# A four-layer graph GRU on one core: the first steps of each layer, the work ahead of the flag and the last statistics put in another order

## The chip, the cores and the metric

The kernel runs on one core of one Trainium2 chip. The metric is the time of one execution on the device in microseconds (us). The kernel before takes 2390.28 us, the median of three runs from 2387.75 to 2390.46.

The engines are named as in the profile: PE multiplies matrices, DVE, ACT and POOL work on tiles of up to 128 partitions, and SP only issues DMAs here. Each engine runs its own instructions in order and waits on semaphores that the others raise.

## The reference

```python
h = x                                              # 50000 nodes x 128
for l in range(4):
    m = h @ weight[l]
    agg = segment_sum(m[src], dst, 50000)          # 75000 edges, sorted by dst; every node has an edge to itself
    gi, gh = agg @ w_ih.T + b_ih, h @ w_hh.T + b_hh
    r = sigmoid(gi_r + gh_r); z = sigmoid(gi_z + gh_z)
    n = tanh(gi_n + r * gh_n)
    h = (1 - z) * n + z * h
y = x + (h + x)
out = (y - mean(y)) / sqrt(var(y) + 1e-5)          # over the 128 features
```

## The kernel before

**Tiling.** The 50000 nodes are cut into 100 blocks of 500. A block's state is kept transposed, 128 features on the partitions and 504 columns (four groups of 125 nodes and one unused column each). Every layer goes over the 100 blocks, one step for a block. Steps are written out for the first ten and the last ten blocks of a layer and looped ten at a time between them. Products are made in fp32r in three passes, so each operand is split into a high part (a rounded copy, made by ACT) and a low part (the difference, made by DVE, or by POOL for the first half of h).

**One block's path.** POOL gathers the rows of the neighbours with three indirect DMAs (`gather`, L555). ACT rounds them (`high_gathered`, L832), DVE makes the remainder (`low_gathered`, L1089), PE sums them over the edges with a 0/1 selection matrix (`sum_edges`, L686), which ACT has widened from bytes (`widen`, L839). DVE adds h (`aggregate`, L1110; the final layer does that on PE instead), ACT and DVE split the result (`high_part` L844, `low_part` L1101). PE makes the products for r, for h's and for the input's part of n, and for z (L698). ACT makes r (`r_gate` L851), DVE `r_times_hn` (L1116) and `n_argument` (L1123), ACT the tanh (`n_gate` L855) and z (`z_gate` L859), DVE `difference` (L1127), `product` (L1133) and `new_state` (L1142). PE turns the new state back to rows (L733), ACT copies it out of PSUM (`rows_out` L865), SP stores it.

**The order.** It is written out by hand, per engine, in a `step` that works on several blocks at once: in step b, DVE and ACT work on r, n and z of block b, but already on the edge sums of block b+2 and on the gathered rows and h of block b+3. The start of a layer (`if first:`) therefore does this work for blocks 0, 1 and 2 before step 0. Steps wait for nothing but their data; every engine's list is fixed.

**Between layers.** A layer's gathers may read any row of the state that the layer before stored, so POOL waits for all stores (`s_store`) before the first of 15 gathers (five blocks). The h columns of the next layer's first five blocks are loaded in the last five steps already.

**Before layer 0** there is a set-up: DVE sorts each block's edges into slots (up to L1064, after which `V_TABLES` is reached), then a check on the edge lists is added up on PE and copied to `flag_i` (L1079). Every engine reads this flag and branches to `fast_path()` or `general_path()`. The inputs take the fast path.

**The end.** In the final layer the sum with x is made two steps later (`ROWLAG`), its statistics in groups of five blocks (`moments`, `squared_difference`, `variance`, then POOL's power L539 and `shift` L1181), and rows are normalised nine blocks later (`OUTLAG`), the first half of a block's columns on ACT (L873), the second half in the last nine blocks on DVE (`last_rows`, L1262).

## Time and profile before

| | |
|---|---|
| median of 3 runs | 2390.28 us |
| lowest, highest | 2387.75, 2390.46 us |
| the profiled execution's own time | 2411.64 us |
| its span, first to last instruction | 2409.9 us |
| mean granted clock of PE | 0.968 |
| PE, DVE busy | 93%, 93% of the span |
| ACT, POOL busy | 78%, 73% |
| set-up (before the flag) | 65.9 us |
| `r_times_hn` of block 0 in layers 0 to 3, at | 87.46, 677.78, 1233.37, 1788.91 us |
| median step of layers 0 to 3 (L1116 to L1116) | 5.65, 5.30, 5.30, 5.78 us |
| last `new_state` of layers 0 to 2, at | 655.88, 1210.76, 1764.82 us |
| last `new_state` to the end of the span | 2390.18 to 2409.9 us |

The profiled execution took 21.4 us more than the median. DVE and PE are busy for 93% of the span; the page's 40 slices fall below 9 tenths of DVE in the first two, at the three changes of layer (slices 11, 20 and 30) and in the last. In the profile "L1116" stands for `r_times_hn`, the first DVE instruction of every step, so the time from one L1116 to the next is the length of a step.

### The profile page before, as it was taken

The page shows a single profiled execution, that of the slowest core. Times are in us where ns is not written, and L with a number is a line of the kernel's source. Part 1 is how long each engine was busy: PE and PEld are TensorE (multiplying, and loading weights), DVE is VectorE, ACT ScalarE, POOL GpSimd, SP SyncE. Part 2 cuts the span into 40 slices and gives each one's busy share as a digit, 9 for nine tenths or more (in the row PEclk, how much of TensorE's full clock was granted, in tenths as well). Part 3 has the DMA queues.
Part 4 walks back from the last instruction along what each step waited for, and adds up shares of the span by engine and source line. Part 5 has one row for each costly group of instructions (what it writes and reads, how often), then busy time and mean ns, then how long its engine had stood idle before and what let it go on. Part 6 is the DMA issues. An engine that isn't in the chain of part 4 may idle for free.

```text
span 2409.9 us, 49779 instructions
## 1 busy us (share of the span) xinstructions
PE 2241.2 (93%) x11832; PEld 1880.0 (78%) x11832; DVE 2250.7 (93%) x4540; ACT 1871.1 (78%) x3592; POOL 1749.2 (73%) x1644
## 2 busy tenths in 40 slices
PE   1799999999879999999969999999969999999996
PEld 0688888888768888888858888888858878778885
DVE  7799999999869999999969999999949999999998
ACT  0588888888758888888758878888847888888886
POOL 1788888778577777777567777777648888888883
PEclk7799999999989999999989999999979999999998
DMA  1355555555535565655535565555534555555553
GB/s 35 104 161 160 155 159 156 159 154 159 153 109 171 170 173 167 173 171 170 167 107 171 169 173 169 170 171 169 171 106 121 152 149 150 149 149 151 152 150 110
DMA packets 277064, 363.68 MB, mean 151 GB/s; under 512 B 107754, under 2 KB 186586, under 8 KB 276980
## 3 DMA queue, kind: packets, MB, share of 16 engines
q1 hardware_dynamic: 238196, 310.43, 43.4%
q0 software_dynamic: 38784, 52.30, 9.2%
q8 instruction: 32, 0.52, 0.1%
q14 instruction: 52, 0.43, 0.1%
HBM read 209.32 MB, written 179.81 MB: 161 GB/s over the span
## 4 chain that ended last, share of the span: by engine, by line
DVE 37%; issue 24%; PE 24%; ACT 10%; DVEq 1%; DMA 1%; POOL 1%; another core or an unknown queue 0%; ACTq 0%; SPq 0%; POOLq 0%
PE pR L698 6%; DVE narg L1123 6%; PE pZ L698 6%; DVE a_lo L1101 5%; DVE diff L1133 4%; DVE diff L1127 4%; DVE bn L1158 3%; PE pHN L698 3%; PE pA L686 3%; DVE y_rows L1151 3%; DVE h_lo L1094 2%; PE pO L733 2%; DVE aggT L1110 2%; DVE narg L1116 2%; DVE sel L1083 2%
## 5 line engine op out<-in xcount | busy, mean ns | idle before, releaser
L555 POOL DMA_INDIRECT gath<-state,idx x900 | 925.7, 1029 | 235.5 <-issue 220.0
L533 POOL TENSOR_TENSOR h_lo<-hT,h_hi 128x252 fp32r<-128x252 f32 (+1 forms) x400 | 351.4, 879 | 260.8 <-DVE diff L1133 124.3
L555 POOL DMA_INDIRECT gath<-in_x_dram,idx x300 | 389.4, 1298 | 124.2 <-issue 121.8
L1116 DVE SCALAR_TENSOR_TENSOR narg<-pHN,bhh,rg 128x504 f32<-128x504 f32 x400 | 293.8, 734 | 17.0 <-ACT rg L851 7.1
L686 PE MATMUL pA<-sel,g_hi 128*128 128x168 f32 x1200 | 280.1, 267 | 31.0 <-DVE g_lo L1089 27.8
L686 PE MATMUL pA<-sel,g_lo 128*128 128x168 f32 x1200 | 292.9, 277 | 0.0
L851 ACT ACTIVATE rg<-pR,bsum 128x504 f32<-128x504 f32 x400 | 274.2, 686 | 21.3 <-PE pR L698 17.7
L1089 DVE TENSOR_TENSOR g_lo<-gath,g_hi 128x384 fp32r<-128x384 f32 x400 | 240.9, 602 | 44.2 <-ACT g_hi L832 42.0
L855 ACT ACTIVATE pA<-narg,bih 128x504 f32<-128x504 f32 x200 | 137.2, 686 | 184.9 <-DVE narg L1123 125.5
L855 ACT ACTIVATE pIN<-narg,bih 128x504 f32<-128x504 f32 x200 | 137.2, 686 | 182.2 <-DVE narg L1123 117.4
L859 ACT ACTIVATE zg<-pZ,bsum 128x504 f32<-128x504 f32 x400 | 270.3, 676 | 5.4 <-remote 4.4
L1133 DVE TENSOR_TENSOR diff<-zg,diff 128x504 f32<-128x504 f32 x400 | 269.1, 673 | 4.4 <-ACT zg L859 3.6
L686 PEld LDWEIGHTS pA<-sel,g_hi 128*128 128x128 f32 x1200 | 231.9, 193 | 49.0 <-issue 32.4
L733 PEld LDWEIGHTS pO<-ident,newT 128*125 128x125 f32 x1400 | 191.2, 188 | 75.1 <-issue 32.0
L839 ACT CAST sel<-sel 128x504 fp32r (+1 forms) x400 | 249.5, 625 | 0.0
L686 PEld LDWEIGHTS pA<-sel,g_lo 128*128 128x128 f32 x1200 | 232.5, 194 | 16.7
L832 ACT CAST g_hi<-gath 128x384 fp32r<-128x384 f32 x400 | 211.0, 527 | 39.7 <-DMA gath<-state,idx 38.3
L733 PE MATMUL pO<-ident,newT 128*125 128x128 f32 x1400 | 222.3, 281 | 14.7 <-DVE newT L1142 13.9
L1110 DVE TENSOR_TENSOR aggT<-pA,hT 128x504 f32<-128x504 f32 x300 | 200.8, 669 | 6.0 <-remote 5.1
L1101 DVE TENSOR_TENSOR a_lo<-aggT,a_hi 128x504 fp32r<-128x504 f32 x300 | 202.3, 674 | 4.1 <-ACT a_hi L844 2.7
L698 PE MATMUL pR<-a_hi,wf_hi 128*128 128x504 f32 x400 | 190.8, 477 | 0.5 <-DVE a_lo L1101 0.4
L844 ACT CAST a_hi<-aggT 128x504 fp32r<-128x504 f32 x300 | 179.5, 598 | 13.4 <-DVE aggT L1110 9.7
(185 smaller groups left out, 6464.0 us busy)
## 6 DMA issues: line engine op xcount, KB each, us to landing
columns<-newT SPq DMA_DIRECT2D x300, 252.0 KB
hT<-columns SPq DMA_DIRECT2D x300, 252.0 KB
state<-o_rows SPq DMA_DIRECT2D x300, 224.0 KB
x_rows<-in_x_dram SPq DMA_DIRECT2D x200, 224.0 KB
out_dram<-o_rows SPq DMA_DIRECT2D x100, 224.0 KB
gath<-state,idx POOLq DMA_INDIRECT x900
state<-o_rows SPq DMA_DIRECT2D x300, 26.0 KB
idx<-edge_src SPq DMA_DIRECT2D x395, 1.5 KB
```

What stands on the lines that cost most here:

```text
L533: nc.gpsimd.tensor_tensor(h_lo[:, u % RING, cols], hT[:, u % RING, cols], h_hi[:, u % RING, cols].bitcast(F32), ALU.subtract).then_inc(s_h ...
L555: pool.indirect_dma_start(out=gath[:, u % RING, j, :], out_offset=None, in_=states[l], in_offset=bass.IndirectOffsetOnAxis(ap=idx[:, u % R ...
L686: last = nc.tensor.matmul(to, rows, cols, start=begins, stop=ends)
L698: last = nc.tensor.matmul(bank, w, xx[:, u % RING, :], start=k == 0, stop=k == len(passes) - 1)
L733: last = nc.tensor.transpose(bank[0:ROWS, k * D:(k + 1) * D], newT[:, u % RING, k * CP:k * CP + ROWS], ident[:, :])
L839: nc.scalar.copy(sel[:, u % 2, :], sel8[:, bass.ds(b, 1), :].rearrange("p o c -> p (o c)")).then_inc(s_sel, 1)
L851: nc.scalar.activation(rg[:, :], pR[:, 0:COLS], ACT.Sigmoid, bias=bsum[:, 0:1]).then_inc(s_r, 1)
L855: nc.scalar.activation(n_bank(u), narg[:, :], ACT.Tanh, bias=bih[:, 2:3]).then_inc(s_n, 1)
L859: nc.scalar.activation(zg[:, :], pZ[:, 0:COLS], ACT.Sigmoid, bias=bsum[:, 1:2]).then_inc(s_z, 1)
L1101: v.tensor_tensor(a_lo[:, u % RING, :], sums_of if summed else aggT[:, :], a_hi[:, u % RING, :].bitcast(F32), ALU.subtract).then_inc(s_alo, 1)
L1116: v.scalar_tensor_tensor(narg[:, :], pHN[:, 0:COLS], bhh[:, 2:3], rg[:, :], ALU.add, ALU.mult).then_inc(s_t1, 1)
L1133: v.tensor_tensor(diff[:, :], zg[:, :], diff[:, :], ALU.mult).then_inc(s_e, 1)
```

## The change

1. **The start of a layer.** Before step 0 only block 0's edge sums are made (gathered rows split, sums, `aggregate`, `high_part`, `low_part`), with block 1's gathered rows split. Block 1's sums stand in step 0 behind the products of r and n, block 2's behind the z product and behind `product` and `z_gate` of block 0, and with them the gathered rows of block 3.
2. **h of the next layer.** `high_h`, `low_h` and `split_h` of the next layer's blocks 0, 1, 2 move into the last three steps of a layer (`on_from`, `PRE = 3`).
3. **Ahead of the flag.** SP loads the first five blocks of x before it waits for the flag; PE turns blocks 0 to 2, ACT copies and rounds them, POOL makes their low parts whole; POOL issues the first 15 gathers when `V_TABLES` is reached; DVE makes block 0's selection bytes between the checks and the flag. Temporaries of the set-up that lay in `hT` move to `y_rows`.
4. **The last statistics.** Those of the last five blocks are made as three (before the sums of the last two blocks) and two (`LATE = 2`). POOL's power and `shift` are divided likewise.

```diff
+PRE = 3
+LATE = 2
...
             def fast_path():
-                for u in range(RING):
-                    load_x(u, u)
...
+            for c in range(PRE):
+                split_h(0, c, c, None, True)
+            for c in range(RING):
+                gather(0, c, c, 0, False)
...
                     def step(i, u, first, last):
                         b = UNROLL * i + u
-                        if first:
-                            if l == 0:
-                                for c in range(RING):
-                                    gather(c, c, 0, False)
-                                    if c < 3:
-                                        split_h(l, c, c)
-                            else:
-                                for c in range(3):
-                                    split_h(l, c, c)
-                                for v in range(RING):
-                                    pool.wait_ge(s_store[v], 32 * TURNS * l)
-                                for c in range(RING):
-                                    gather(c, c, 0, True)
-                        if exists(i, u, 3):
-                            nb, nu, _ = after(i, u, 3)
-                            split_h(l, nb, nu, l * NB + b if exists_before(i, u, 1) else None)
+                        if first and l:
+                            for v in range(RING):
+                                pool.wait_ge(s_store[v], 32 * TURNS * l)
+                            for c in range(RING):
+                                gather(l, c, c, 0, True)
+                        coming = on_from(l, i, u, PRE)
+                        if coming:
+                            split_h(*coming[:3], l * NB + b if exists_before(i, u, 1) else None)
...
+            pe.wait_ge(s_v, V_WEIGHTS)
+            for c in range(PRE):
+                turn_h(c, c, s_xld[c % RING], 2, c == 0)
...
                             sum_edges(l, 0, 0, start)
+                        r_and_n_products(l, b, u, start,
+                                         l * NB + b - 1 if l or exists_before(i, u, 2) else None,
+                                         l < L - 1 and (l > 0 or exists_before(i, u, PRE)))
+                        if first:
                             sum_edges(l, 1, 1, False)
-                        r_and_n_products(l, b, u, start,
-                                         l * NB + b - 1 if l or exists_before(i, u, 2) else None, l < L - 1)
-                        if exists(i, u, 2):
+                        elif exists(i, u, 2):
                             sum_edges(l, *after(i, u, 2)[:2], False)
                         z_product(l, b, u, start)
+                        if first:
+                            sum_edges(l, 2, 2, False)
...
                         normal(i, u, 0)
+                        if first:
+                            high_part(l, 1, 1, final)
                         n_gate(l, b, u)
...
                         normal(i, u, 1)
+                        if first:
+                            high_gathered(2, 2, TURNS * l + 1)
+                            widen(l, 2, 2)
+                            high_part(l, 2, 2, final)
+                            high_gathered(3, 3, TURNS * l + 1)
+                            widen(l, 3, 3)
...
+            for j in range(TILES):
+                select(0, 0, j)
             dve.wait_ge(s_flag, 1)
...
+                        summed = after(i, u, 1 if first else 2)[:2] if exists(i, u, 2) else None
+                        if not final and summed:
+                            aggregate(l, *summed)
...
-                        if exists(i, u, 3):
+                        if not first and exists(i, u, 3):
                             low_gathered(l, *after(i, u, 3)[:2])
-                            if not final:
-                                low_h(l, *after(i, u, 3)[:2])
-                        if exists(i, u, 2):
-                            low_part(l, *after(i, u, 2)[:2], final)
+                        coming = on_from(l, i, u, PRE)
+                        if coming and coming[0] < L - 1:
+                            low_h(*coming[:3])
+                        if summed:
+                            low_part(l, *summed, final)
                         product(l, b, u)
...
+                        if first:
+                            low_gathered(l, 2, 2)
+                            if not final:
+                                aggregate(l, 2, 2)
+                            low_part(l, 2, 2, final)
+                            low_gathered(l, 3, 3)
...
-                        for k in range(ROWLAG, 0, -1):
+                        ahead = slice(RING, UNROLL - LATE), TURNS - 1
+                        late = slice(UNROLL - LATE, UNROLL), TURNS
+                        moments(*ahead, NB - LATE)
+                        squared_difference(*ahead)
+                        variance(*ahead)
+                        for k in range(LATE, 0, -1):
                             remainder(NB - k, UNROLL - k, GROUPS - 1)
                             row_stats(NB - k, UNROLL - k)
-                        whole = slice(RING, UNROLL), TURNS - 1
-                        moments(*whole, NB)
+                        moments(*late, NB)
...
```

ACT at the start of layer 1 before: block 2's widened matrix (`sel`) and gathered rows, block 1's sums, r of block 0 (`rg`), and so on to r of block 1 in the last row.

```order
L839 CAST sel<-sel 128x504
L832 CAST g_hi<-gath 128x384
L844 CAST a_hi<-aggT 128x504
L851 ACTIVATE rg<-pR,bsum 128x504
L828 CAST h_hi<-hT 128x504
L832 CAST g_hi<-gath 128x384
L839 CAST sel<-sel 128x504
L855 ACTIVATE pIN<-narg,bih 128x504
L844 CAST a_hi<-aggT 128x504
L859 ACTIVATE zg<-pZ,bsum 128x504
L851 ACTIVATE rg<-pR,bsum 128x504
```

And now, from the gathered rows of block 1 to r of block 1:

```order
L857 CAST g_hi<-gath 128x384
L876 ACTIVATE rg<-pR,bsum 128x504
L853 CAST h_hi<-hT 128x504
L869 CAST a_hi<-aggT 128x504
L880 ACTIVATE pIN<-narg,bih 128x504
L884 ACTIVATE zg<-pZ,bsum 128x504
L857 CAST g_hi<-gath 128x384
L864 CAST sel<-sel 128x504
L869 CAST a_hi<-aggT 128x504
L857 CAST g_hi<-gath 128x384
L864 CAST sel<-sel 128x504
L876 ACTIVATE rg<-pR,bsum 128x504
```

Between r of block 0 and r of block 1 ACT had three rounded copies of h, g and the sums, one matrix to widen, tanh and z. It now has h of block 3, the sums of block 1 ahead of the tanh, and behind z the rows of blocks 2 and 3, their two matrices and the sums of block 2.

DVE there before, from block 1's `aggregate` on, with `r_times_hn` of blocks 0 and 1 as the rows `narg<-pHN`:

```order
L1110 TENSOR_TENSOR aggT<-pA,hT 128x504
L1101 TENSOR_TENSOR a_lo<-aggT,a_hi 128x504
L1116 SCALAR_TENSOR_TENSOR narg<-pHN,bhh,rg 128x504
L1123 TENSOR_TENSOR narg<-pIN,narg 128x504
L1110 TENSOR_TENSOR aggT<-pA,hT 128x504
L1127 TENSOR_TENSOR diff<-hT,pIN 128x504
L1089 TENSOR_TENSOR g_lo<-gath,g_hi 128x384
L1094 TENSOR_TENSOR h_lo<-hT,h_hi 128x252
L1101 TENSOR_TENSOR a_lo<-aggT,a_hi 128x504
L1133 TENSOR_TENSOR diff<-zg,diff 128x504
L1116 SCALAR_TENSOR_TENSOR narg<-pHN,bhh,rg 128x504
```

And now, from `r_times_hn` of block 0 to that of block 1:

```order
L1149 SCALAR_TENSOR_TENSOR narg<-pHN,bhh,rg 128x504
L1156 TENSOR_TENSOR narg<-pIN,narg 128x504
L1143 TENSOR_TENSOR aggT<-pA,hT 128x504
L1160 TENSOR_TENSOR diff<-hT,pIN 128x504
L1127 TENSOR_TENSOR h_lo<-hT,h_hi 128x252
L1134 TENSOR_TENSOR a_lo<-aggT,a_hi 128x504
L1166 TENSOR_TENSOR diff<-zg,diff 128x504
L1122 TENSOR_TENSOR g_lo<-gath,g_hi 128x384
L1143 TENSOR_TENSOR aggT<-pA,hT 128x504
L1134 TENSOR_TENSOR a_lo<-aggT,a_hi 128x504
L1122 TENSOR_TENSOR g_lo<-gath,g_hi 128x384
L1149 SCALAR_TENSOR_TENSOR narg<-pHN,bhh,rg 128x504
```

Block 1's `aggregate` and `a_lo` moved behind `r_times_hn` of block 0, and behind `product` (`diff<-zg,diff`) there are four more instructions ahead of block 1's `r_times_hn`.

DVE at the very end of the final layer, from the last new state on, before:

```order
L1142 TENSOR_TENSOR newT<-diff,pA 128x504
L1151 SCALAR_TENSOR_TENSOR y_rows<-x_rows,pO 125x512
L1158 BN_STATS bn<-y_rows 125x6 x4
L1151 SCALAR_TENSOR_TENSOR y_rows<-x_rows,pH 125x512
L1158 BN_STATS bn<-y_rows 125x6 x4
L1163 TENSOR_TENSOR mv<-bn 125x20
L1164 SCALAR_TENSOR_TENSOR mv<-bn 125x20
L1165 TENSOR_TENSOR mv<-bn 125x20
L1169 SCALAR_TENSOR_TENSOR mv<-mv 125x20
L1175 SCALAR_TENSOR_TENSOR veps<-mv 125x20
L1262 TENSOR_SCALAR o_rows<-y_rows,rstd,nmr 125x128 x8
```

And now:

```order
L1175 TENSOR_TENSOR newT<-diff,pA 128x504
L1196 TENSOR_TENSOR mv<-bn 125x12
L1197 SCALAR_TENSOR_TENSOR mv<-bn 125x12
L1198 TENSOR_TENSOR mv<-bn 125x12
L1202 SCALAR_TENSOR_TENSOR mv<-mv 125x12
L1208 SCALAR_TENSOR_TENSOR veps<-mv 125x12
L1184 SCALAR_TENSOR_TENSOR y_rows<-x_rows,pO 125x512
L1191 BN_STATS bn<-y_rows 125x6 x4
L1184 SCALAR_TENSOR_TENSOR y_rows<-x_rows,pH 125x512
L1191 BN_STATS bn<-y_rows 125x6 x4
L1196 TENSOR_TENSOR mv<-bn 125x8
```

Five small instructions on 12 columns now stand ahead of the sums with x (`y_rows`) of the last two blocks, and those on 20 columns have become ones on 8.

## Rows read from the trace of the kernel before

**Rows 1.** The page, its first line.

```profile
span 2409.9 us, 49779 instructions
```

**Rows 2.** Timeline of DVE at the start of layer 1: start us, duration us, instruction [idle before].

```profile
654.28 0.68 DVE L1127 TENSOR_TENSOR diff<-hT,pA 128x504 f32<-128x504 f32 x1 [0.75 <-ACT pA L855]
655.06 0.68 DVE L1133 TENSOR_TENSOR diff<-zg,diff 128x504 f32<-128x504 f32 x1
...
667.51 0.56 DVE L1089 TENSOR_TENSOR g_lo<-gath,g_hi 128x384 fp32r<-128x384 f32 x1 [6.38 <-ACT g_hi L832]
671.37 0.56 DVE L1089 TENSOR_TENSOR g_lo<-gath,g_hi 128x384 fp32r<-128x384 f32 x1 [3.30 <-ACT g_hi L832]
671.84 0.68 DVE L1110 TENSOR_TENSOR aggT<-pA,hT 128x504 f32<-128x504 f32 x1
673.20 0.68 DVE L1101 TENSOR_TENSOR a_lo<-aggT,a_hi 128x504 fp32r<-128x504 f32 x1 [0.68 <-ACT a_hi L844]
...
677.78 0.74 DVE L1116 SCALAR_TENSOR_TENSOR narg<-pHN,bhh,rg 128x504 f32<-128x504 f32 x1
...
682.97 0.68 DVE L1110 TENSOR_TENSOR aggT<-pA,hT 128x504 f32<-128x504 f32 x1 [2.94 <-remote]
...
688.03 0.74 DVE L1116 SCALAR_TENSOR_TENSOR narg<-pHN,bhh,rg 128x504 f32<-128x504 f32 x1 [1.81 <-ACT rg L851]
```

**Rows 3.** Timeline of ACT, the same stretch.

```profile
672.55 0.61 ACT L844 CAST a_hi<-aggT 128x504 fp32r<-128x504 f32 x1 [1.22 <-issue]
...
677.01 0.68 ACT L851 ACTIVATE rg<-pR,bsum 128x504 f32<-128x504 f32 x1
```

**Rows 4.** Timeline of PE, the same stretch.

```profile
668.21 0.48 PE L686 MATMUL pA<-sel,g_hi 128*128 128x168 f32 x1 [10.38 <-DVE g_lo L1089]
...
674.13 0.76 PE L698 MATMUL pR<-a_hi,wf_hi 128*128 128x504 f32 x1
```

**Rows 5.** Timeline of DVE at the starts of layers 0, 2 and 3.

```profile
93.69 0.73 DVE L1116 SCALAR_TENSOR_TENSOR narg<-pHN,bhh,rg 128x504 f32<-128x504 f32 x1
...
1242.86 0.74 DVE L1116 SCALAR_TENSOR_TENSOR narg<-pHN,bhh,rg 128x504 f32<-128x504 f32 x1 [0.91 <-ACT rg L851]
...
1793.00 0.69 DVE L1123 TENSOR_TENSOR narg<-pIN,narg 128x504 f32<-128x504 f32 x1 [3.34 <-remote]
...
1799.18 0.74 DVE L1116 SCALAR_TENSOR_TENSOR narg<-pHN,bhh,rg 128x504 f32<-128x504 f32 x1 [0.47 <-ACT rg L851]
```

**Rows 6.** Timeline of POOL at the starts of layers 0 to 3.

```profile
67.36 1.04 POOL L555 DMA_INDIRECT gath<-in_x_dram,idx  x1 [46.94 <-issue]
...
81.56 0.73 POOL L533 TENSOR_TENSOR h_lo<-hT,h_hi 128x252 fp32r<-128x252 f32 x1
...
661.85 1.01 POOL L555 DMA_INDIRECT gath<-state,idx  x1 [0.15 <-issue]
...
1216.62 1.01 POOL L555 DMA_INDIRECT gath<-state,idx  x1 [0.54 <-issue]
...
1767.98 3.69 POOL L533 TENSOR_TENSOR h_lo<-hT,h_hi 128x504 fp32r<-128x504 f32 x3 [21.03 <-ACT h_hi L828]
1771.80 1.01 POOL L555 DMA_INDIRECT gath<-state,idx  x1
```

**Rows 7.** Timeline of DVE in the set-up and in the first step of layer 0.

```profile
64.06 0.17 DVE L1064 CAST edge_src<-pA 128x21 int32<-128x21 f32 x1
...
81.63 1.22 DVE L1101 TENSOR_TENSOR a_lo<-aggT,a_hi 128x504 fp32r<-128x504 f32 x1 [0.68 <-issue]
```

**Rows 8.** Timeline of DVE at the end of the program.

```profile
2393.89 0.20 DVE L1163 TENSOR_TENSOR mv<-bn 125x20 f32<-125x20 f32 x1
...
2394.67 2.13 DVE L1262 TENSOR_SCALAR o_rows<-y_rows,rstd,nmr 125x128 f32<-125x128 f32 x8
```

**Rows 9.** Windows: us, busy us of PE, PEld, DVE, ACT, POOL, then PEclk, DMA share, GB/s.

```profile
673.00:675.00 2.00, 2.00 (x8) 1.73 (x8) 0.68 (x1) 0.92 (x3) 1.45 (x2) 0.50 0.15 25
2398.00:2400.00 2.00, 0.00 (x0) 0.00 (x0) 1.54 (x7) 1.29 (x4) 0.39 (x1) 0.50 0.85 251
```

More of the change, by code:

```diff
@@ L363, in load_x @@
                     sp.dma_start(x_rows[part, u % RING, :], rows_of(x, b)[part, :]).then_inc(s_xld[u % RING], 16)
+            for u in range(RING):
+                load_x(u, u)
             def indices(b, u):
@@ L448, in general_path @@
             def general_path():
+                sp.wait_ge(s_pH, PRE)
+                for u in range(RING):
+                    sp.wait_ge(s_xld[u], 32)
                 for l in range(L):
@@ L644, in _, with at_least, turn_h @@
                 nc.tensor.matmul(bank[:, 0:3 * D], wT[:, l, :], wihT[:, :], start=True, stop=True).then_inc(s_wf, 1)
+            def at_least(s, value, start):
+                if not start:
+                    pe.wait_ge(s, value)
+            def turn_h(g, u, loaded, loads, start):
+                pe.wait_ge(loaded, 16 * loads)
+                at_least(s_hhi, g, start)
+                for k in range(RPP):
+                    last = nc.tensor.transpose(pH[:, k * CP:k * CP + ROWS], x_rows[:, u % RING, k * D:(k + 1) * D],
+                                               ident[0:ROWS, 0:ROWS])
+                last.then_inc(s_pH, 1)
+            pe.wait_ge(s_v, V_WEIGHTS)
+            for c in range(PRE):
+                turn_h(c, c, s_xld[c % RING], 2, c == 0)
             pe.wait_ge(s_v, V_SLOTS)
@@ L821, in copy_turned @@
                 nc.scalar.copy(h_hi[:, u % RING, :], pH[:, 0:COLS]).then_inc(s_hhi, 1)
+            for c in range(PRE):
+                copy_turned(c, c)
             def high_h(l, b, u, loads):
@@ L1085, in select @@
                                 None, ALU.is_equal).then_inc(s_sel8, 1)
+            for j in range(TILES):
+                select(0, 0, j)
+            dve.wait_ge(s_flag, 1)
+            done(v.tensor_copy(flag_i[0:1, 0:1], pR[0:1, 0:1]))
+            assert steps[0] == V_FLAG
             def low_gathered(l, b, u):
@@ L1316, in one @@
                         if l == L - 1:
[L1317 removed]
+                            residual(b, 0, 1, b + 2)
                             row_stats(b, 0)
```

155 lines of the change are left out of this document (72 added, 83 removed).

## The prediction

> **What bounds the kernel now.** I read the page first: DVE is busy for 93% of a span of 2409.9 us [rows 1], with PE beside it, and the slices that fall below are the set-up, the three changes of layer and the end. In between, a step takes 5.3 to 5.7 us (99 steps lie between the L1116 of a layer's first and last block), and the change leaves the order of such a step alone. So only five places can move: the set-up with the start of layer 0, the starts of layers 1, 2 and 3, and the end. For them I read the timelines of DVE, ACT, PE and POOL. The yardstick is the stretch from the first gather G of a layer to block 1's L1116, behind which both kernels go on in the same order. It is 688.03 - 661.85 = 26.2 us in layer 1, 1242.86 - 1216.62 = 26.2 in layer 2 and 1799.18 - 1771.80 = 27.4 in layer 3 [rows 2, 5, 6].
>
> Those stretches hold waits that no order explains: in layer 1 `aggregate` of block 2 waits 2.94 us for a signal that the trace can't name, and block 1's L1116 another 1.81 behind ACT [rows 2]; in layer 3 `n_argument` waits 3.34 [rows 5]. All are for PE, whose matmuls are recorded as long done. Without them block 1's L1116 would come at G + 21.4 in layer 1 (26.2 - 2.94 - 1.81; I take the same for layer 2) and at about G + 22.4 in layer 3 (27.4 - 3.34, and a second wait like the 1.81). The Trainium skill (Perfetto Trace Analysis, Tensor Engine Instruction) says that the profile's end of a matmul is computed, not observed; by that rule the waiters are to be believed and PE's rows are not. The trace agrees: it is DVE and ACT that stand still.
>
> The profiled execution took 2411.6 us and the median is 2390.3, so 21.4 us are missing from the runs that are timed. Three starts with some 4.9 us of such waits would be 14.7 of them. I reckon with differences only, and add them to the median.
>
> **The start of layers 1 to 3.** Times from G, intervals from rows of layer 1. Before: block 0's g_lo at 5.7, its sums on PE at 6.4 (667.51, 668.21), ready at about 8.0; but `aggregate` stands behind block 1's g_lo (671.37, which waited for its gather) and starts at 10.0. Then 0.71 to a_hi, 0.65 to a_lo, 0.93 to the r product at 12.3, 2.88 to r, 0.77 to L1116 at 15.9 [rows 2 to 4].
> Now `aggregate` goes at 8.0, a_hi 8.7, a_lo 9.4, the r product 10.3: 2.0 us earlier. r comes at 13.2, block 0's L1116 at 14.1 (it waits for h's part of n, at the half clock that the windows show here [rows 9]). That is 1.8 us won.
> Then the new order charges. PE makes block 1's sums only behind block 0's n product: 15.1 to 15.9. `aggregate` 16.0, a_hi 16.7, and the tanh stands behind that a_hi: 17.2. `difference` 17.9, h_lo and a_lo of block 1 to 19.4, `product` 19.4, g_lo of block 2 20.0 (ACT's copy for it stands behind z), PE's sums 20.7 to 21.4, `aggregate` 21.5, a_hi 22.2. On ACT the rows and the matrix of block 3 follow (0.4 and 0.5), so r of block 1 starts at 23.6, though its product is ready at 23.0, and L1116 at 24.4. Each step of this sum is 0.6 to 0.7 us, the spacing of DVE's and ACT's rows, or 0.93 into PE. It is a single file through four engines, where before block 2's sums were under way beside block 0's gates.
> So block 1's L1116 moves from 21.4 to 24.4: **+3.0 us** each in layers 1 and 2. In layer 3 there is no `aggregate`, but two more matmuls in each sum; the same count gives 24.6 against 22.4, **+2.2**. If the unnamed waits occur in both kernels in like size, they drop out of the difference.
>
> **h of the next layer.** ACT's copies lie in waits for DVE. DVE's h_lo costs 0.33 us behind the last `difference`, where 0.1 to 0.2 was free (0.78 from 654.28 to 655.06 for work that is spaced 0.6) [rows 2]: +0.2 in layers 0 and 1, nothing in layer 2, where POOL makes them whole. The two steps before wait for r by 0.3 and hide it. What it frees is POOL ahead of G. In layer 2 the gather still waited 0.54 us after POOL was free, so the stores set it; in layer 1 it came right behind POOL's work but no earlier from the last new state than in layer 2, so I take 0 in both (up to 0.5 won). In layer 3 POOL worked 3.69 us and G came 7.0 us after the last new state instead of 5.9 [rows 6]: **-1.1**, with 0 and -1.6 as bounds.
>
> **The set-up and layer 0.** Tables are ready at 64.23 (64.06 + 0.17) [rows 7], and POOL gathers at once: G = 64.4 instead of 67.36 [rows 6]. The 15 gathers are no longer broken by h_lo. With 24.4 from G and 0.3 for bytes made in the step, L1116 of block 1 would come at 89.1, against 93.69 [rows 5]. Against this stand 2.5 MB of x that are now loaded while the windows of the edge list are gathered, three POOL instructions beside DVE's sorting, and 0.7 us of bytes ahead of the flag (hidden: gathers don't wait for the flag, and ACT needs them only at 67). The first two aren't in the trace; the bounds are 0 and some 3 us, and I take 0.7: **-3.9**.
> On the second: a_lo took 1.22 us beside POOL's h_lo and 0.68 elsewhere in this line [rows 6, 7], so an h_lo of POOL costs DVE 0.5. The Trainium skill (SBUF — State Buffer, section SBUF: two separate sides) calls the port of DVE and POOL an exclusive lock for a DVE instruction with two SBUF inputs. By the rule three h_lo of 1.3 us would block DVE for up to 3.9 us of the set-up; by the row 1.5. But the sorting reads one tile at a time, so by the rule, too, the cost can be nothing.
>
> **The end.** Between the last new state and the first stored block, DVE made one set of statistics, 0.78 us (2393.89 to 2394.67) [rows 8]. Now there are two sets, the first ahead of the last two blocks' sums with x, and the first `last_rows` stands behind both: it starts 0.8 us later. POOL's power of the three blocks ends earlier, but it was not the limit: once begun, the nine stores keep the DMAs at 0.85 busy and 251 GB/s [rows 9], 2.3 MB in 9 us, and the last blocks wait for a slot in `o_rows`, so the whole train shifts: **+0.8** (between -1, if the earlier shift closes gaps, and +1.5).
>
> **The clock.** Block 1's sums done, PE has nothing from 17.4 to 20.7 us after G. If the clock falls there, r's and h's products of block 1 are made at the lower level: 3.65 us instead of about half (674.13 to 677.78) [rows 2, 4], at most 1.8 us a start. I take 0.3 for each of four: **+1.2**.
>
> **Sum.** -3.9 + 2 x (3.0 + 0.2) + 2.2 - 1.1 + 0.8 + 1.2 = +5.6 us: 2390.3 + 5.6 = **2395.9 us**. A profiled execution would come out at about 2417 if the unnamed waits recur.
>
> **Rivals.**
> A, faster. The unnamed waits are a price of PE's dense start behind two sums, they are in the timed runs too, and the new start, which is thinner on PE, is free of them. For: they occur at all three starts and never in layer 0, where POOL's gathers were interrupted. Against: the same train of 15 gathers and the same loops remain. Then the yardstick goes from 26.2 to 24.4 twice and from 27.4 to 24.6: -3.9 - 2 x 1.6 - 2.8 - 1.1 + 0.8 + 1.2 = -9.0, **2381.3 us**. It decides as soon as the waits in the timed runs exceed 3 us a start.
> B, no difference. The waits are in both, but the longer single file lies partly under them (a signal that comes at G + 21 is late for the old order and early enough for the new): some +1.3 instead of +3.0 a start: -3.9 + 3.0 + 0.9 - 1.1 + 0.8 + 0.6 = +0.3, **2390.6 us**.
> C, slower still. The x loads and POOL's work delay the sorting by 3 us and layer 0 wins 1.5 instead of 3.9, and the clock falls at every start (1.0 each): +5.6 + 2.4 + 2.8 = +10.8, **2401.1 us**.
>
> **Chances.** The forecast 0.50, A 0.23, B 0.17, C 0.10. What can't be told from no change is 0.2%, 4.8 us. The forecast's own range is 2392 to 2400, so it counts 0.6 as slower and 0.4 as the same; A 0.85 faster; B 0.8 the same, the rest on both sides; C slower. Together faster 0.22, same 0.36, slower 0.42. The range that leaves out two in ten runs from 2382 to 2401.
>
> **What would show it.** In the profile of the changed kernel: block 0's L1116 1.8 us nearer to G in layers 1 to 3, and block 1's L1116 at G + 24.4 or, with unnamed waits, later; r of block 1 on ACT behind the matrix of block 3; G of layer 0 at 64.4 to 66, and of layer 3 5.9 us after the last new state; the first `last_rows` 4.5 to 5.5 us after the last new state, where it was 4.5. Wrong would be: block 1's L1116 at G + 22 or less, or unnamed waits gone where the old kernel has them and a time below 2386.

## The result and the profile after

The changed kernel takes 2403.72 us, the median of six runs from 2400.81 to 2404.23; the kernel before takes 2389.31 beside it (six runs, 2387.75 to 2390.46). The ratio is 1.0058, with a 95% interval of 1.0048 to 1.0068: 14.4 us slower. I had forecast 5.6 us slower, and the range ended at 2401.

Its profiled execution took 2400.81 us, so it is one of the timed ones. The profiled one of the kernel before (2411.64) is not: it has 21 us that the timed runs don't have. It most likely ran on another chip. The later runs were made in five comparisons, each on another chip. In the runs of the result (whose chip isn't recorded) and in two of the five, the kernel before took 2387 to 2390 us; in the other three 2404 to 2417. I call the chips of the first group X and those of the second Y. No chip is known to have been used twice, so a difference between chips and one between occasions aren't told apart. A trace of the kernel before on an X chip was taken in the third comparison (2388.54 us, span 2386.8), and the two kernels are compared by that one.

The page of the changed kernel, its first line:

```profile
span 2399.0 us, 49806 instructions
```

Timeline of DVE at the start of layer 1 in the changed kernel (start, duration, instruction, idle time before it and who ended it); it answers to [rows 2]. L1149 is `r_times_hn`, L1143 `aggregate`, L1134 `low_part`, L1122 `low_gathered`, L1166 `product`:

```profile
662.08 0.56 DVE L1122 TENSOR_TENSOR g_lo<-gath,g_hi 128x384 fp32r<-128x384 f32 x1 [10.40 <-ACT g_hi L857]
664.46 0.68 DVE L1143 TENSOR_TENSOR aggT<-pA,hT 128x504 f32<-128x504 f32 x1 [1.83 <-PE pA L704]
...
670.49 0.74 DVE L1149 SCALAR_TENSOR_TENSOR narg<-pHN,bhh,rg 128x504 f32<-128x504 f32 x1 [3.52 <-PE pHN L716]
...
673.87 0.68 DVE L1160 TENSOR_TENSOR diff<-hT,pIN 128x504 f32<-128x504 f32 x1 [1.26 <-ACT pIN L880]
...
675.39 1.65 DVE L1166 TENSOR_TENSOR diff<-zg,diff 128x504 f32<-128x504 f32 x1
676.97 0.54 DVE L1122 TENSOR_TENSOR g_lo<-gath,g_hi 128x384 fp32r<-128x384 f32 x1
679.34 0.68 DVE L1143 TENSOR_TENSOR aggT<-pA,hT 128x504 f32<-128x504 f32 x1 [1.83 <-PE pA L704]
680.70 0.68 DVE L1134 TENSOR_TENSOR a_lo<-aggT,a_hi 128x504 fp32r<-128x504 f32 x1 [0.68 <-ACT a_hi L869]
...
683.10 0.74 DVE L1149 SCALAR_TENSOR_TENSOR narg<-pHN,bhh,rg 128x504 f32<-128x504 f32 x1 [1.24 <-PE pHN L716]
```

G, the start of a layer's first gather, from the timeline of POOL in the changed kernel, for layers 0, 1 and 3 [rows 6]:

```profile
65.80 1.04 POOL L569 DMA_INDIRECT gath<-in_x_dram,idx  x1 [30.51 <-DVE sums L1104]
...
656.44 1.01 POOL L569 DMA_INDIRECT gath<-state,idx  x1 [8.64 <-issue]
...
1763.50 1.01 POOL L569 DMA_INDIRECT gath<-state,idx  x1 [8.34 <-issue]
```

And the same place in the kernel before on an X chip, DVE's rows and then POOL's:

```profile
672.56 0.74 DVE L1116 SCALAR_TENSOR_TENSOR narg<-pHN,bhh,rg 128x504 f32<-128x504 f32 x1
673.41 0.68 DVE L1123 TENSOR_TENSOR narg<-pIN,narg 128x504 f32<-128x504 f32 x1
674.01 0.67 DVE L1110 TENSOR_TENSOR aggT<-pA,hT 128x504 f32<-128x504 f32 x1
...
678.61 0.73 DVE L1116 SCALAR_TENSOR_TENSOR narg<-pHN,bhh,rg 128x504 f32<-128x504 f32 x1
```

```profile
656.49 1.01 POOL L555 DMA_INDIRECT gath<-state,idx  x1 [0.15 <-issue]
```

Block 0's L1116 stands at G + 14.0 (670.49 - 656.44) in the changed kernel and at G + 16.1 in the one before. Block 1's stands at G + 26.7 (683.10 - 656.44) against G + 22.1. The new start wins 2 us on the first block and gives back 6.6 on the second. The unnamed waits of [rows 2, 5] are in neither of these two traces, nor in the five others taken on X chips. The windows tell what PE did in that stretch; first the changed kernel, then the one before (columns as in [rows 9]):

```profile
674.00:677.00 3.00, 0.00 (x0) 0.00 (x0) 3.00 (x5) 1.35 (x3) 2.52 (x4) 0.92 0.25 40
677.00:680.00 3.00, 2.34 (x9) 2.19 (x10) 1.17 (x3) 0.00 (x0) 2.39 (x3) 0.50 0.32 99
680.00:683.00 3.00, 3.00 (x9) 2.37 (x8) 1.18 (x3) 2.64 (x6) 0.54 (x1) 0.50 0.14 29
```

```profile
672.00:674.00 2.00, 2.00 (x13) 1.78 (x12) 1.84 (x3) 1.16 (x3) 1.39 (x3) 1.00 0.08 19
674.00:676.00 2.00, 2.00 (x10) 1.64 (x9) 1.23 (x3) 2.00 (x5) 1.68 (x2) 1.00 0.17 43
676.00:679.00 3.00, 3.00 (x18) 2.59 (x17) 3.00 (x6) 2.65 (x5) 2.53 (x3) 1.00 0.49 115
```

In the rows of PE the pause is longer than the empty window. It lasts from the end of block 0's z product (672.75 + 0.39) to block 2's sums at 677.66, 4.5 us:

```profile
672.75 0.39 PE L716 MATMUL pZ<-h_hi,whh_lo 128*128 128x504 f32 x1
677.66 0.48 PE L704 MATMUL pA<-sel,g_hi 128*128 128x168 f32 x1 [4.52 <-DVE g_lo L1122]
...
679.00 0.69 PE L716 MATMUL pR<-a_hi,wf_hi 128*128 128x504 f32 x1
...
682.44 0.62 PE L716 MATMUL pHN<-h_hi,whh_lo 128*128 128x504 f32 x1
```

In the pause the granted clock falls from 1.0 to 0.5 (from 2.4 to 1.2 GHz), and block 2's sums and block 1's products for r and h are made at that level. Block 1's L1116 waits 1.24 us for the last of these. In the kernel before PE is never empty there and stays at 1.0.

The two spans differ by 12.2 us. By stages, changed against before (both X), us:

| | before | changed | difference |
|---|---|---|---|
| block 1's L1116 of layer 0, at | 93.75 | 93.12 | -0.6 |
| G after the last new state, layers 1, 2, 3 | 5.98, 5.98, 6.66 | 5.44, 5.82, 5.84 | -1.5 |
| G to block 1's L1116, layers 1, 2, 3 | 22.12, 22.10, 22.09 | 26.66, 26.55, 27.17 | +14.1 |
| block 1's L1116 to the last new state, four layers | | | +1.2 |
| last new state to the end | 20.44 | 19.49 | -0.95 |

The starts of layers 1 to 3 make the whole loss. The end can't be told from nothing: with the last statistics undivided, four traces on X chips have 20.4, 19.4, 19.2 and 19.7 us from the last new state to the end. The six timed runs of the changed kernel fall into two groups, two at 2400.8 and four at 2403.7 to 2404.2; the trace is of the first, and what the second has more stays open. So the trace accounts for 12.2 of the 14.4 us.

### The profile page after: what moved, and what is told of

It is laid out like the page before. It is cut to its first block, busy times and chain, and to the rows that moved or that the text cites. A ratio compares the mean times of both kernels' runs of the same rounds, so it can differ in the third digit from the quotient of the medians.

```text
span 2399.0 us, 49806 instructions
## 1 busy us (share of the span) xinstructions
PE 2234.8 (93%) x11832; PEld 1892.6 (79%) x11832; DVE 2247.0 (94%) x4543; ACT 1877.9 (78%) x3592; POOL 1710.5 (71%) x1645
## 4 chain that ended last, share of the span: by engine, by line
DVE 38%; PE 28%; issue 25%; ACT 6%; DVEq 1%; DMA 1%; POOL 0%; SPq 0%; ACTq 0%; POOLq 0%
DVE narg L1156 8%; PE pR L716 7%; DVE a_lo L1134 7%; PE pZ L716 7%; PE pA L704 4%; PE pHN L716 3%; DVE diff L1160 3%; DVE h_lo L1127 3%; DVE diff L1166 3%; DVE bn L1191 3%; ACT pA L880 3%; ACT pIN L880 3%; DVE y_rows L1184 3%; DVE narg L1149 2%; PE pO L752 2%
## 5 line engine op out<-in xcount | busy, mean ns | idle before, releaser
L569 POOL DMA_INDIRECT gath<-in_x_dram,idx x300 | 352.2, 1174 | 108.7 <-issue 73.6
L1149 DVE SCALAR_TENSOR_TENSOR narg<-pHN,bhh,rg 128x504 f32<-128x504 f32 x400 | 293.2, 733 | 23.9 <-PE pHN L716 18.0
L1122 DVE TENSOR_TENSOR g_lo<-gath,g_hi 128x384 fp32r<-128x384 f32 x400 | 240.7, 602 | 35.2 <-ACT g_hi L857 35.2
L1166 DVE TENSOR_TENSOR diff<-zg,diff 128x504 f32<-128x504 f32 x400 | 271.9, 680 | 0.8 <-DVE diff L1160 0.5
L752 PEld LDWEIGHTS pO<-ident,newT 128*125 128x125 f32 x1400 | 199.8, 187 | 50.9 <-DVE newT L1175 28.4
L857 ACT CAST g_hi<-gath 128x384 fp32r<-128x384 f32 x400 | 209.9, 525 | 27.7 <-DMA gath<-state,idx 25.9
L752 PE MATMUL pO<-ident,newT 128*125 128x128 f32 x1400 | 215.0, 276 | 9.0 <-DVE newT L1175 8.8
L1143 DVE TENSOR_TENSOR aggT<-pA,hT 128x504 f32<-128x504 f32 x300 | 200.1, 667 | 9.9 <-PE pA L704 9.9
L1134 DVE TENSOR_TENSOR a_lo<-aggT,a_hi 128x504 fp32r<-128x504 f32 x300 | 202.0, 673 | 4.1 <-ACT a_hi L869 4.1
```

The source lines that it names most:

```text
L569: pool.indirect_dma_start(out=gath[:, u % RING, j, :], out_offset=None, in_=states[l], in_offset=bass.IndirectOffsetOnAxis(ap=idx[:, u % R ...
L752: last = nc.tensor.transpose(bank[0:ROWS, k * D:(k + 1) * D], newT[:, u % RING, k * CP:k * CP + ROWS], ident[:, :])
L1134: v.tensor_tensor(a_lo[:, u % RING, :], sums_of if summed else aggT[:, :], a_hi[:, u % RING, :].bitcast(F32), ALU.subtract).then_inc(s_alo, 1)
L1149: v.scalar_tensor_tensor(narg[:, :], pHN[:, 0:COLS], bhh[:, 2:3], rg[:, :], ALU.add, ALU.mult).then_inc(s_t1, 1)
L1166: v.tensor_tensor(diff[:, :], zg[:, :], diff[:, :], ALU.mult).then_inc(s_e, 1)
```

## The experiments

"Part 1" to "part 4" are the numbered parts of the change. A kernel named by its parts has the others undone. X and Y say which kind of chip it ran on: one that takes 2388 us for the kernel before, or one that takes 2408 to 2412.

**The kernel before once more.** No edit.

> The kernel before once more, unchanged, for a trace of an execution at its usual time. Theory S (the starts of the layers): the usual execution has none of the unnamed waits, its time is 2388 to 2391, and the L1116 of block 1 stands 21.4 us behind the first gather in layers 1 and 2 and 22 to 23 us in layer 3, where the profile before had 26.2, 26.2 and 27.4; the changed kernel has 26.7, so its start costs some 5 us in each of three layers, 15 in all. Rival T (the steps): the starts are as long as in the profile before (26 to 27 us), and the usual execution gains its 20 us in the steps between, 0.05 us a step. Rival L (layer 0): most of the difference to 2411 lies in layer 0, whose steps had 6.3 us of hiccups.

2413.69 us: a Y chip, as the 21 runs beside it on that chip (2408 to 2417). Its block 1's L1116 stood 26.9 us behind G in layer 1, with an `aggregate` that waited 2.99 us for an unnamed signal. So my "usual execution" was wrong for this chip, and the waits are no accident of one profile. All traces on Y chips have them, and none of the seven on X chips.

**Part 1 undone.** On PE (ACT and DVE likewise):

```diff
                             sum_edges(l, 0, 0, start)
+                            sum_edges(l, 1, 1, False)
                         r_and_n_products(l, b, u, start,
...
-                        if first:
-                            sum_edges(l, 1, 1, False)
-                        elif exists(i, u, 2):
+                        if exists(i, u, 2):
                             sum_edges(l, *after(i, u, 2)[:2], False)
                         z_product(l, b, u, start)
-                        if first:
-                            sum_edges(l, 2, 2, False)
```

> The changed kernel with the start of a layer (part 1) in the old order: sums of blocks 0 and 1 before the first products, block 2's in step 0. Theory S: the loss goes with it. What is left are the earlier gathers (0.5 us in each of three layers, 1.6 in layer 0) and the h parts: 2384 to 2388 us, ratio 0.998 to 0.9995 of before, against 1.006 for the changed kernel. Rival H: the h parts of the next layer, moved into steps on which DVE or ACT is already late, cost the 14 us; then this stays at 2400 to 2404. Rival P: half each, 2394 to 2398.

Y: 2417.0 against 2412.0, ratio 1.0022 (1.0013 to 1.0031). That is neither S nor H. The ratio is the one that rival P (half each) would have, but the loss that stays, 5 us, did not come back on X chips (parts 2 and 3 below).

**Part 4 undone,** and **parts 1 and 4 undone.** One `moments`, `variance` and `root` over the last five blocks instead of two.

> The changed kernel with the last statistics undivided (part 4 undone). Theory S: the end is worth nothing either way, since the last new state stands 19.5 us before the end in the changed kernel and 19.7 before: 2403 to 2404 us. My prediction's step had the division cost 0.8: 2402.9. Rival E: the division is what slows the last layer (its steps had 27 us of hiccups against 20): 2396 to 2398.

> The changed kernel with parts 1 and 4 undone: only the h parts of the next layer and the work ahead of the flag are new. Theory S: within 0.5 us of the kernel with part 1 alone undone, 2384 to 2388 us. By my prediction's steps: 2389.3 - 3.9 + 0.4 - 1.1 = 2384.7, and 0.8 less than with the statistics divided. Rival H: 2400 or more.

Y: 2429.9, ratio 1.0064 (1.0050 to 1.0078), and 2418.9, ratio 1.0025 (1.0015 to 1.0034). The statistics can't be told from nothing (1.0022 and 1.0025). Between these two kernels part 1 costs 11 us.

**Part 1 alone,** and **the changed kernel once more.**

> The kernel before with part 1 alone (the new order at the start of a layer). Theory S: part 1 is the whole of the loss that came on the chip of the first comparison (+14.4), so this takes 1.005 to 1.007 of before, +12 to +17 us, and in its trace block 0's L1116 comes 1.5 to 2 us nearer to the first gather and block 1's stands 26.5 to 27.5 us behind it in layers 1 and 2 when no signal of PE is late, up to 30 when some are. My prediction's step had +3.0 a start, 9 to 10 in all. Rival I: part 1 is harmless by itself and costs only together with the moved h parts: ratio under 1.002.

> The changed kernel once more, unchanged, on the chip of these runs. If this chip runs the kernel before in 2389, 2400 to 2404 is expected; if it takes 2412, 2426 to 2432 (1.006 to 1.008 of before) by theory S, since the kernel with the old statistics took 2430 there. Rival E (the division of the statistics gains or costs something at the end): 5 us or more away from that.

Y, another chip (before 2411.2): 2422.6, ratio 1.0051 (1.0038 to 1.0064), and 2426.3, ratio 1.0066 (1.0054 to 1.0079). Part 1 alone makes most of the loss or all of it (the intervals overlap), so rival I, that it costs only together with the moved h parts, is out.

**PE kept busy in its pause,** in the changed kernel:

```diff
+            def keep_busy(read, times):
+                pe.wait_ge(s_r, read)
+                for k in range(times):
+                    nc.tensor.matmul(pR[:, 0:3 * D], whh_hi[:, 0:D], whh_hi[:, 0:3 * D], start=True, stop=True)
...
                         z_product(l, b, u, start)
                         if first:
+                            keep_busy(l * NB + 1, 22)
                             sum_edges(l, 2, 2, False)
```

> The changed kernel with 22 more matmuls of 384 columns on PE behind the z product of block 0 of each layer, where PE had nothing for 4.5 us; their results are read by nobody. Theory K (the clock): the granted clock stays at 1.0 until block 1's products are made, these take 2.8 instead of 5.0 us and block 1's L1116 comes 2 to 2.5 us earlier in each of four layers, 8 to 10 us in all against the changed kernel. Theory F (single file): PE's clock does not matter, since the order of the instructions on DVE and ACT sets L1116; the gain is under 2 us in all. The matmuls may also end late and push the sums of block 2: then it is slower.

Y: 2422.5, ratio 1.0049 (1.0033 to 1.0064), against 1.0066 for the changed kernel. The intervals overlap, so this is inconclusive; theory K had 8 to 10 us.

**PE kept busy ahead of the layer,** in the kernel before: 56 such matmuls ahead of block 0's sums.

> The kernel before with 56 more matmuls of 384 columns on PE ahead of block 0's sums in layers 1 to 3, where PE had nothing for 10 us; their results are read by nobody. Theory K: r and h's products of block 0 are made at the full clock, 1.8 us earlier, and the unnamed waits behind them shrink or go where they occur: 5 us less in all on a chip that runs the kernel before in 2389, up to 15 less on one that takes 2412. Rival U: the unnamed waits have nothing to do with PE's clock and stay as they are, and L1116 of block 1 is set by the gathers of block 2: no change within 2 us.

Y: 2412.7, ratio 1.0010 (1.0000 to 1.0020). In layer 1 the clock was back at 0.5 from 668 on, ahead of block 0's products, and two unnamed waits of 2.0 and 3.0 us stood behind these. It tells nothing of theory K, since it didn't reach what it was for.

**Part 3 alone, part 2 alone.**

> The kernel before with part 3 alone (x turned and the first gathers begun ahead of the flag). With parts 2 and 3 together the kernel took 2418.9 against 2412.0, +6.9. Theory P3: the loss belongs to part 3, through layer 0, whose steps from block 1 to block 99 took 559.8 and 560.4 us in the two kernels with parts 2 and 3 and 556.1 in the one before: this takes +4 to +7 here as well, and its layer 0 again 559 to 561. Rival P2: part 3 alone is free or a gain, 0 to -4 us. My prediction's step: -3.9.

> The kernel before with part 2 alone (h of the next layer split in the last three steps). Theory P3: nothing, -2 to +1 us. Rival P2: the loss belongs here, +4 to +7 us. My prediction's step: 0.4 - 1.1 = -0.7.

X: 2384.0 against 2387.95, ratio 0.9983 (0.9974 to 0.9992), and 2386.0, ratio 0.9992 (0.9983 to 1.0001). So both are gains on an X chip: -4.0, and -1.9 with an interval that reaches zero, where the prediction had -0.7. The -3.9 that the expectation quotes was forecast for parts 1 and 3 together in layer 0, so its likeness to -4.0 is chance (see below). The trace of part 3 alone, DVE at block 1's L1116 in layer 0, which was at 93.75 before:

```profile
89.06 0.74 DVE L1143 SCALAR_TENSOR_TENSOR narg<-pHN,bhh,rg 128x504 f32<-128x504 f32 x1
```

**A mixed start.** Block 0 first as in the change, but block 2 beside block 0's gates. On DVE (ACT: `high_gathered` and `widen` of block 2 between r and tanh):

```diff
+                        if first:
+                            if not final:
+                                aggregate(l, 1, 1)
+                            low_gathered(l, 2, 2)
...
+                            difference(l, b, u)
+                            low_part(l, 1, 1, final)
+                            product(l, b, u)
+                            if not final:
+                                aggregate(l, 2, 2)
+                            low_gathered(l, 3, 3)
...
```

> The kernel before with a third order at the start of a layer: block 0's sums alone ahead of the first products, as in the changed kernel, but block 2's gathered rows split between r and tanh of block 0 on ACT and between n_argument and difference on DVE, so that its sums follow block 0's z product on PE at once, and aggregate of block 2 stands right behind product of block 0. Theory S (the single file and the pause of PE cost the 5 us a start): block 0's L1116 at 14 to 14.5 us behind the first gather, block 1's at 20.5 to 22, and 0 to 8 us less than before where before has no late signals. Rival U: PE's signals come late whatever the order, as soon as its first products are made; then block 1's L1116 is at 26 us or more again and the time within 3 us of before.

> The kernel before, unchanged, for its trace on the chip of these runs. If the time is near 2389, block 1's L1116 stands 21.4 us behind the first gather in layers 1 and 2 by my reading; if it is near 2412, 26 to 27.

X: 2389.1, ratio 1.0005 (0.9996 to 1.0014), and 2388.5 for the kernel before. Block 1's L1116 stood at G + 21.3 in layers 1 and 2 and 21.9 in layer 3, 0.8 and 0.2 us earlier than before; in layer 0, which keeps the old gathers and selection bytes here, at G + 27.5 instead of 26.4. Rival U had 26 or more in layers 1 to 3 and is out on this chip. The places are those of theory S, but no gain in time came of them.

**On a third Y chip** (before 2408.0): PE's pause filled with 27 matmuls; parts 2, 3 and 4 with the mixed start in layers 1 to 3; part 1 undone; the changed kernel.

> The changed kernel with 27 more matmuls of 384 columns on PE behind the z product of block 0 of each layer (22 before), whose results are read by nobody. Theory K (the clock): on a chip that runs the kernel before in 2388, where no signal of PE is late, the granted clock stays at 1.0 until block 1's products are made; block 1's L1116 comes at 24.3 to 25 us behind the first gather in layers 1 and 2 (26.6 in the changed kernel), and the time is 6 to 9 us below the changed kernel's. Theory F (single file alone): within 2 us of it. On a chip that takes 2411, where PE's signals come late, the additional work may only make them later (the first try: 4 us less than the changed kernel, with intervals that touch).

> The kernel before with parts 2, 3 and 4 and, in layers 1 to 3 alone, the mixed start of e10 (layer 0 keeps the old order). From the separate measurements of the last four runs: -3.9 for part 3, -1.9 for part 2, -0.8 for each of two starts and -0.3 for the third (21.3 and 21.9 instead of 22.1 us from the first gather to block 1's L1116), about 0 for part 4: 2380 us on a chip with 2388 before, ratio 0.9965. Rival D (the gains don't add, since an earlier start only meets the gathers of block 3 or 4): 2383 or more.

> The changed kernel with part 1 alone undone, once more. On a chip with 2388 before, the separate measurements give -3.9 - 1.9 = 2382; where it was run first (2412 before) it was 5 us slower than before. If this chip has 2411 before, 2415 to 2418.

> The changed kernel once more, for the comparison with the three others on the same chip: 2401 to 2404 where before takes 2388, 2425 to 2428 where it takes 2411.

2417.8, 2406.2, 2411.2 and 2418.9 us, ratios 1.0043 (1.0029 to 1.0057), 0.9990 (0.9981 to 0.9999), 1.0012 (1.0003 to 1.0021) and 1.0042 (1.0029 to 1.0056). The filled pause does nothing here. DVE of the changed kernel in layer 0 on this chip, and then block 2's `aggregate` in layer 1 with the pause filled:

```profile
85.48 0.68 DVE L1143 TENSOR_TENSOR aggT<-pA,hT 128x504 f32<-128x504 f32 x1 [3.03 <-remote]
...
92.42 0.68 DVE L1166 TENSOR_TENSOR diff<-zg,diff 128x504 f32<-128x504 f32 x1 [3.39 <-ACT zg L884]
```

```profile
692.55 0.68 DVE L1149 TENSOR_TENSOR aggT<-pA,hT 128x504 f32<-128x504 f32 x1 [3.48 <-remote]
```

All wait for PE (z came late to ACT), whose matmuls are recorded as done. In the last one block 2's sums are recorded at the full clock and end at 690.1, but DVE gets them 2.4 us later. So what the held clock wins is lost again in front of `aggregate`. Whether the additional matmuls make the signal later was not tested.

**The filled pause and the mixed start on an X chip** (before 2387.7).

> The changed kernel with the 27 matmuls in PE's pause once more. On a chip that takes 2411 the addition changed nothing (2417.8 against 2418.9). On a chip with 2388 before, theory K: 2394 to 2398 (the changed kernel 2403.7 there), block 1's L1116 at 24.3 to 25 us behind the first gather in layers 1 and 2 and PE's granted clock at 1.0 until then. Theory F: 2401 to 2404, L1116 at 26 us or more.

> Parts 2, 3 and 4 with the mixed start in layers 1 to 3 once more. It took 0.999 of before where before takes 2408. On a chip with 2388 before: 2380, and block 1's L1116 at 21.3 to 21.9 us behind the first gather in layers 1 to 3. If the gains don't add: 2383 or more.

2396.9, ratio 1.0038 (1.0024 to 1.0052), and 2381.9, ratio 0.9973 (0.9963 to 0.9984). PE with the pause filled, windows as above, G at 654.78:

```profile
674.00:677.00 3.00, 3.00 (x20) 2.75 (x19) 2.26 (x3) 0.00 (x0) 2.52 (x4) 1.00 0.37 101
677.00:680.00 3.00, 3.00 (x15) 2.22 (x14) 1.83 (x3) 1.87 (x4) 1.97 (x2) 1.00 0.13 32
```

DVE there, block 2's `aggregate` and block 1's L1116 (here L1155):

```profile
675.71 0.55 DVE L1128 TENSOR_TENSOR g_lo<-gath,g_hi 128x384 fp32r<-128x384 f32 x1
677.41 0.68 DVE L1149 TENSOR_TENSOR aggT<-pA,hT 128x504 f32<-128x504 f32 x1 [1.16 <-PE pA L704]
...
680.35 0.74 DVE L1155 SCALAR_TENSOR_TENSOR narg<-pHN,bhh,rg 128x504 f32<-128x504 f32 x1 [0.42 <-ACT rg L882]
```

The clock stays at 1.0, in the starts of the other layers too. From block 2's g_lo to its `aggregate` it takes 1.70 us instead of 2.37 (676.97 to 679.34), from there to L1116 2.94 instead of 3.76: 1.5 us. As a slower product and `a_lo` take a part back, L1116 comes at G + 25.6, 25.9 and 25.9 in layers 1 to 3, 1.1, 0.6 and 1.2 us earlier, and in layer 0 1.1 earlier. That is 4.1 in all by the traces. The ratios (1.0058 - 1.0038, of 2388) give 4.8, but they are of two chips and their intervals touch, so by themselves they show little. The time is where theory K had it, L1116 is up to 0.9 us later than its 24.3 to 25, and the traces give more than the 2 us that F allowed. What is left above before with the clock held is 3.5 to 3.9 us in each of layers 1 to 3: the single file, and in it DVE instructions that are stretched beside POOL.

The last kernel is the fastest that I ran. Its time lies between the two forecasts (2380 if the gains add, 2383 or more if not). DVE at the start of its layer 1 (L1160 is `r_times_hn`, G at 651.39):

```profile
665.61 0.74 DVE L1160 SCALAR_TENSOR_TENSOR narg<-pHN,bhh,rg 128x504 f32<-128x504 f32 x1 [3.68 <-PE pHN L716]
...
672.74 0.73 DVE L1160 SCALAR_TENSOR_TENSOR narg<-pHN,bhh,rg 128x504 f32<-128x504 f32 x1
```

Block 0 comes as early as in the change (G + 14.2), block 1 at G + 21.4. So the early first block is harmless; what costs is the row of steps behind it. The kernel is 5.9 us faster than before on an X chip and 1.8 on a Y chip. That is no more than parts 2 and 3 give when their two results are added (4.0 + 1.9): a gain from the mixed start itself isn't shown in the times, only that the loss of part 1 is gone.

## Why the prediction was wrong

The failed step is the start of a layer, in layers 1 to 3 by its clock term and its stretched instructions, in layer 0 by the same and by a later G. The sign and the kind of the cost, a single file for the second block, were right; the sizes were not. By places, forecast and measured (spans, both X), us:

| | forecast | measured |
|---|---|---|
| G to block 1's L1116, layers 1 to 3, with the clock | +9.1 | +14.1 |
| layer 0 to block 1's L1116, with the clock | -3.6 | -0.6 |
| h of the next layer and G of layers 1 to 3 | -0.7 | -1.2 |
| the steps between | 0 | +0.9 |
| the end | +0.8 | -0.95 |

These add up to +5.6 and +12.2. The other 2 us of the 14.4 are in the four timed runs of the upper group and stay unexplained.

- **The old start.** The step took the unnamed waits off the profile and had block 1's L1116 at G + 21.4 (22.4 in layer 3, where taking 3.34 and 1.81 off 27.4 gives 22.2). It is at G + 22.1 in all three. The error is small: it made the new start look 0.7 us worse in two layers and 0.3 better in the third.
- **The new start, block 0.** G + 14.1 forecast, 14.0, 14.5 and 14.6 measured. Right.
- **The new start, block 1.** G + 24.4 forecast, 26.7 measured in layer 1. `product` starts 0.4 earlier than forecast (18.95 for 19.4), but it took 1.65 us instead of 0.68, beside an h_lo of POOL, so that g_lo of block 2 is at 20.5 for 20.0. From there to `aggregate` it takes 2.4 us for 1.5, since PE's sums take 1.5 at the half clock (677.66 to 679.20) where 0.7 was forecast. From `aggregate` to L1116 it takes 3.8 for 2.9, since the products for r and h take 4.1 us (679.00 to 683.06). With the pause filled the last two come out as forecast, 1.7 and 2.9.
- **The clock.** The pause was foreseen, 3.3 us of it, and [rows 9] showed the low level. To take 0.3 us a start had no reason. By the two traces it costs 1.1, 1.1, 0.65 and 1.2 us in layers 0 to 3, 4.1 where 1.2 was counted. The bound of 1.8 a start holds.
- **Stretched instructions.** With the clock held, block 1's L1116 in layers 1 to 3 comes 11.1 us later than before in all, for 8.2 forecast. Between the L1116 of blocks 0 and 1, DVE's instructions beside POOL's h_lo take 1.1, 1.2 and 1.6 us more than elsewhere in that kernel, and 0.6, 0.5 and 1.2 more in the kernel before. My sum for the new start had none. The difference, 1.6 us, is an estimate of what that left out of the 2.9; the rest, 1.3 us, I have not placed.
- **Layer 0.** -3.9 was forecast for parts 1 and 3 together, -0.6 measured. Part 3 alone moves block 1's L1116 from 93.75 to 89.06: G comes 1.5 us earlier (65.86 for 67.32), and from G to L1116 it is 23.2 us instead of 26.4, as the 15th gather is issued 18.6 instead of 21.8 us behind G when no h_lo is in between. The new start then takes L1116 to 93.12. By my own terms part 3 should have given more (64.4 + 21.4 + 0.3 = 86.1) and the new start taken 3.0 of it. I had put L1116 at G + 24.7 and G at 64.4; they were 27.3 (1.0 of it the stretched `product` of 1.66 us, 1.1 the clock) and 65.8. The last table was written at 64.83 instead of 64.02 (kernel before, X): one copy of the sorting takes 1.45 us for 0.49 beside the first of POOL's h_lo. That fits the 0.7 that I had taken. POOL then began 0.8 us behind the tables, where I had 0.
- **Layer 3.** G came 5.84 us after the last new state instead of 6.66: -0.8 for -1.1. The start cost +5.1 for +2.2.
- **The end.** The first `last_rows` stands 5.1 us after the last new state (2379.51 to 2384.61) where it was 4.5: the +0.6 is there, for +0.8. But the whole train did not shift with it: 19.5 us to the end, and 19.2 to 20.4 with the statistics undivided. What sets the end was not found.
- **The rivals.** A (the waits are in the timed runs and vanish) fell: on X chips they are in neither kernel, on Y chips in both. B fell. C came nearest (+10.8) and had the clock term about right (1.0 a start), but it put the rest of its loss into sorting that is delayed by 3 us; that was 0.8, and layer 0 lost its gain by the new start.

**Open.** Parts 2 and 3 without part 1 win 5.9 us on an X chip if their two results are added. On two Y chips they lose 3 to 7, with part 4 in two of the three runs. On the first of these chips, block 1's L1116 of layer 0 stands at 94.1 with and without the earlier gathers. The steps of layer 0 behind it take 558.8 to 560.4 us, against 556.1 and 557.9 in the two traces of the kernel before that have unnamed waits; on the second of the chips there is no such trace. Why PE's signals come late on Y chips was not found.

## What to carry over

When a pipeline is filled again, count the way of the second block as carefully as that of the first: to start the first early is worth nothing if the second then goes alone through every engine. Where a new order leaves PE without work for some microseconds, charge the work behind the pause at the half clock; here it was about 1 us a start. And before terms of the profile are dropped because the timed runs are shorter, get a trace of a run of the usual length; here a difference between chips, or occasions, stood behind them.

## What the runs showed of the hardware

- **Chips differ by 1%.** The kernel before took 2386.8 to 2390.5 us on X chips and 2403.6 to 2416.7 on the three Y chips. On Y chips waiters stand for up to 6.7 us where PE takes up work again, for matmuls recorded as done. The longest is block 0's L1116 in layer 3 of the first Y trace, at 1794.57, when the last matmul that it needs is recorded to end at 1789.09. In some steps of layer 0 L1116 waits up to 0.7 us for such a signal.
- **A pause lowers the clock for the work behind it.** In 4.5 us without a matmul the granted clock fell from 1.0 to 0.5 (677 to 683 us); work that nobody reads held it at 1.0 and brought block 1's L1116 4.1 us forward over four starts.
- **DVE beside POOL.** `product` took 1.65 us beside POOL's h_lo of 0.73 us; in 397 of the 400 steps it took 0.9 or less. The 1 us more is more than POOL's whole instruction, where the prediction had reckoned with 0.5 from [rows 7]. DVE and POOL in layers 1 and 3 of the changed kernel:

```profile
675.39 1.65 DVE L1166 TENSOR_TENSOR diff<-zg,diff 128x504 f32<-128x504 f32 x1
675.76 0.73 POOL L549 TENSOR_TENSOR h_lo<-hT,h_hi 128x252 fp32r<-128x252 f32 x1
...
1782.79 2.07 DVE L1166 TENSOR_TENSOR diff<-zg,diff 128x504 f32<-128x504 f32 x1
1783.05 1.25 POOL L549 TENSOR_TENSOR h_lo<-hT,h_hi 128x504 fp32r<-128x504 f32 x1
```

Both times `product` ends 0.55 us behind POOL's instruction. The Trainium skill (SBUF — State Buffer, section SBUF: two separate sides) has a lock that the one that starts first holds for its whole instruction, while the other waits. The trace agrees that one is held up until the other is done, but not on which: by the recorded starts DVE's came first, by 0.37 and 0.26 us. In the set-up only one instruction paid. A copy on DVE took 1.45 us beside the first of three h_lo, for 0.49 before; beside the other two the sorting went on at the pace of the kernel before. That copy reads one tile, which my prediction had as the case in which nothing might be lost.

```profile
29.63 1.45 DVE L1061 COPY y_rows<-newT 100x480 f32<-100x480 f32 x1
```

```profile
29.45 1.29 POOL L549 TENSOR_TENSOR h_lo<-hT,h_hi 128x504 fp32r<-128x504 f32 x1 [9.20 <-ACT h_hi L843]
```
